# Attention on one NeuronCore: single-bank rings for trial and score products, exponentials 512 wide

## The reference

```
xn = layer_norm(x, norm_w, norm_b)
q = (xn @ q_w + q_b).reshape(Bx, Tx, H, -1)
k = (xn @ k_w + k_b).reshape(Bx, Tx, H, -1)
att = jnp.einsum('bnhl,bmhl->bnmh', q, k)
att = att + (1.0 - mask) * -1000000.0
att = jax.nn.softmax(att, axis=2)
v = ((xn @ v_w + v_b) * src_mask[:, :, None]).reshape(Bx, Tx, H, -1)
y = jnp.einsum('bnmh,bmhl->bnhl', att, v).reshape(Bx, Tx, Dx)
...
h = layer_norm(y, sb_norm_w, sb_norm_b) * (1.0 + scale) + shift
h = jax.nn.silu(h) @ out_w + out_b
return x + h
```

## Time and profile before

| | us |
|---|---|
| median of three runs | 2032.05 |
| the three runs | 2032.08, 2032.05, 2026.07 |
| profiled execution, first to last instruction | 2030.2 |
| lead stretch, 1509.4 to 1572.9 | 63.5 |
| 54 steps with trials, 1572.9 to 1954.2 | 381.3 |
| ten steps without trials, 1954.2 to 2003.8 | 49.6 |
| the end, from 2003.8 | 26.4 |

### The profile page before, as it was taken

How to read it: one execution, slowest core, us unless ns; L and a number is a source line. 1 busy time by engine, 2 the same in 40 slices (tenths; PEclk the granted TensorE clock), 3 DMA queues, 4 the chain that set the end, 5 groups by cost and what they waited for, 6 DMA issues and landing times. The chain is left out here.

```text
span 2030.2 us, 32413 instructions
## 1 busy us (share of the span) xinstructions
PE 1909.2 (94%) x12312; PEld 1341.5 (66%) x12312; DVE 1601.3 (79%) x2109; ACT 1415.3 (70%) x2410; POOL 1047.9 (52%) x603
## 2 busy tenths in 40 slices
PE   6989999999999999989999999899988999999997
PEld 3664999759995799689965998699842222222223
DVE  5565899669995999789976997799969777777642
ACT  3326999379973999699928996998542666665665
POOL 3021799409991599469922997399626000002000
PEclk9989899989999999999999999999988999999998
DMA  5032211102111111011100111111011111111000
GB/s 193 1 102 76 68 58 58 48 27 65 57 52 53 37 58 58 22 44 56 55 11 18 58 58 39 48 58 58 27 24 39 33 31 33 33 33 33 9 22 21
DMA packets 57546, 95.18 MB, mean 47 GB/s; under 512 B 14951, under 2 KB 23559, under 8 KB 55982
## 3 DMA queue, kind: packets, MB, share of 16 engines
q1 hardware_dynamic: 55854, 88.90, 14.3%
q0 software_dynamic: 1536, 4.20, 0.7%
HBM read 73.55 MB, written 6.91 MB: 40 GB/s over the span
## 5 line engine op out<-in xcount | busy, mean ns | idle before, releaser
L973 POOL TENSOR_TENSOR A<-A 128x1024 f32<-128x1024 f32 x384 | 895.7, 2388 | 231.5 <-ACT small L885 161.5
L893 ACT ACTIVATE A<-A,negA 128x512 f32<-128x512 f32 x768 | 549.6, 718 | 30.5 <-DVE A L954 23.6
L954 DVE TENSOR_TENSOR_SCAN A<-A,small,PS 128x512 f32<-128x512 f32 x384 | 453.8, 1258 | 8.2 <-ACT A L893 5.1
L954 DVE TENSOR_TENSOR_SCAN A<-A,PS 128x512 f32<-128x512 f32 x384 | 431.8, 1198 | 21.7 <-PE PS L806 10.9
L831 PE MATMUL PS<-ident,A 128*128 128x128 f32 x3072 | 402.8, 274 | 13.4 <-POOL A L973 10.0
L1499 DVE TENSOR_REDUCE A<-PS 128x1 f32<-128x512 f32 x512 | 324.8, 682 | 101.2 <-PE PS L1486 99.4
L1733 ACT ACTIVATE A<-PS 128x1024 f32<-128x1024 f32 x256 | 260.0, 1023 | 181.7 <-PE PS L1697 179.9
L806 PE MATMUL PS<-A 128*128 128x128 f32 x3072 | 384.8, 277 | 0.2
L806 PEld LDWEIGHTS PS<-A 128*128 128x128 f32 x3072 | 364.0, 193 | 3.6 <-DVE A L954 0.6
L831 PEld LDWEIGHTS PS<-ident,A 128*128 128x128 f32 x3072 | 348.4, 142 | 21.4 <-POOL A L973 13.5
L870 ACT ACTIVATE A<-A,small 128x512 f32<-128x512 f32 x320 | 229.4, 717 | 13.2 <-PE PS L812 13.2
(11 more groups left out here) (194 smaller groups left out, 1841.8 us busy)
## 6 DMA issues: line engine op xcount, KB each, us to landing
A<-scrc SPq DMA_DIRECT2D x192, 256.0 KB, 3.1
A<-A SPq DMA_DIRECT2D x360, 32.0 KB
scr<-A SPq DMA_DIRECT2D x4, 1024.0 KB, 5.0
W<-in_wa SPq DMA_DIRECT2D x2, 1536.0 KB, 9.8
X<-in_x SPq DMA_DIRECT2D x4, 512.0 KB, 5.7
scr<-W SPq DMA_DIRECT2D x128, 1.5 KB
out<-X SPq DMA_DIRECT2D x4, 512.0 KB, 2.9
W<-in_w SPq DMA_DIRECT2D x1, 1984.0 KB, 7.4
```

The source lines that it names most:

```text
L893: e.activation(A_B[i % 4], r.DT[:, dt, ci * 512:(ci + 1) * 512], ACT.Exp, scale=negA[:, r.n, dt * 16 + s:dt * 16 + s + 1]).then_inc(*decay ...
L954: e.tensor_tensor_scan(h, a, u, init, ALU.mult, ALU.add).then_inc(*scanned.up((q, i)))
L973: e.tensor_tensor(h, h, CB[k % 2].unsqueeze(1).broadcast_to([128, 2, 512]), ALU.mult).then_inc(*weighed.up((q, pair)))
```

## The change

The trials get three single banks (0 to 2), the scores three single banks (3 to 5). Every score product of 512 columns now signals for itself, and every Exp is 512 wide: 512 of them in place of 256 of 1024. A weighing block waits for the Exps of its own half c alone, and an Exp waits for the weighing of its own half. In a step the weighing block stands behind the score products of head j = 1 and j = 3, no longer between the first trial and the first score product of that head. The transposed results take two single banks of the trial ring, at the end of the step mt = 1 rather than behind its first head, and VectorE normalises them in two halves, at the end of that step too. VectorE's copy of the upper bank moves from behind head 3 of mt = 0 to behind head 0 of mt = 1. The output projections of the first batch (`tail_due` 2 to 5) take banks of the trial ring, its transposes those of the score ring. In the lead stretch the projections rotate over five banks, not six.

```
-        first, six, doubles = Banks(0, 2), Banks(2, 6), Banks(2, 2, 2)
+        first, five, scores = Banks(0, 3), Banks(3, 5), Banks(3, 3)
...
         def weigh_t(e, w, u, mt, c):
...
                 if mt == 0 and u:
-                    w.wait_ge(*act.at(("lower", u - 1)))
-                    w.wait_ge(*dve.at(("upper", u - 1)))
-                w.wait_ge(*act.at(("weights", u, mt, j)))
+                    w.wait_ge(*(dve.at(("upper", u - 1)) if c else act.at(("lower", u - 1))))
+                w.wait_ge(*act.at(("weights", u, mt, j, c)))
...
         def normalise_t(e, w, u):
-            take(w, ("turned", u), doubles)
...
+            for c in range(2):
+                o = take(w, ("turned", u, c), first)
+                w.wait_ge(*(dve.at(("upper", u)) if c else act.at(("lower", u))))
+                for q in range(4):
+                    t = e.transpose(o[:, q * 128:(q + 1) * 128], PVs[:, c * 512 + q * 128:c * 512 + (q + 1) * 128], ident[:, :])
+                t.then_inc(*pe.up(("turned", u, c)))
...
         def layer3_t(e, w):
...
                     for c in range(2):
                         ahead_t(e, w, LEAD + 32 * u + 4 * mt + j, (c,))
-                        if c == 0:
-                            if last and j % 2:
-                                weigh_t(e, w, *last, j // 2)
-                            take(w, key, doubles)
+                        o = take(w, ("score", u, mt, j, c), scores)
                         w.wait_ge(*transfer(f"max_row{sl}").at(k))
...
-                    t.then_inc(*pe.up(key))
-                    if j == 0 and u and mt == 1:
-                        normalise_t(e, w, u - 1)
+                                 start=True, stop=True).then_inc(*pe.up(("score", u, mt, j, c)))
+                    if last and j % 2:
+                        weigh_t(e, w, *last, j // 2)
+                if u and mt == 1:
+                    normalise_t(e, w, u - 1)
...
         def layer3_s(e, w):
...
-                    e.activation(PX[mt % 2][j], PS[:, i:i + 2, :].rearrange("p a b -> p (a b)"), ACT.Exp).then_inc(*act.up(("weights", u, mt, j)))
-                    banks.give(key, act.now())
+                    for c in range(2):
+                        key = ("score", u, mt, j, c)
+                        w.wait_ge(*pe.at(key))
+                        if step >= 2:
+                            w.wait_ge(*pe.at(("weighed", (step - 2) // 8, (step - 2) % 8, c)))
+                        e.activation(PX[mt % 2][j][:, c * 512:(c + 1) * 512], bank(key), ACT.Exp).then_inc(*act.up(("weights", u, mt, j, c)))
+                        banks.give(key, act.now())
```

More of the change, by code:

```diff
@@ L1347, in program @@
         units = [(b, g) for b in range(NB) for g in range(H // HQ)]
-        first, six, doubles = Banks(0, 2), Banks(2, 6), Banks(2, 2, 2)
-        rings = [banks, first, six, doubles]
+        first, five, scores = Banks(0, 3), Banks(3, 5), Banks(3, 3)
+        rings = [banks, first, five, scores]
         def layer2_done(w):
@@ L1539, in normalise_t @@
         def normalise_t(e, w, u):
-            take(w, ("turned", u), doubles)
[L1541 to L1545, removed]
+            for c in range(2):
[4 more added lines that the diff above has]
+                t.then_inc(*pe.up(("turned", u, c)))
         def normalise_s(e, w, u):
-            w.wait_ge(*pe.at(("weighed", u, TB - 1, 1)))
+            w.wait_ge(*pe.at(("weighed", u, TB - 1, 0)))
             if u:
-                w.wait_ge(*pe.at(("turned", u - 1)))
+                w.wait_ge(*pe.at(("turned", u - 1, 0)))
             e.activation(PVs[:, 0:512], PV[:, 0, :], ACT.Copy).then_inc(*act.up(("lower", u)))
@@ L1560, in normalise_v @@
             b, g = units[u]
[L1561 to L1567, removed]
-            y = Yt[:, b * TB:(b + 1) * TB, HQ * 16 * g:HQ * 16 * (g + 1)].rearrange("p q (j e) -> p q j e", j=HQ)
-            e.tensor_tensor(y, f4[:, :, :, 0:16], RC.unsqueeze(3).broadcast_to([128, TB, HQ, 16]), ALU.mult).then_inc(*dve.up(("y3", u)))
-            banks.give(("turned", u), dve.now())
+            y = Yt[:, b * TB:(b + 1) * TB, HQ * 16 * g:HQ * 16 * (g + 1)].rearrange("p q (j e) -> p q j e", j=HQ)
+            for c in range(2):
+                f4 = bank(("turned", u, c)).rearrange("p (q j e) -> p q j e", j=HQ, e=32)
+                r = RC[:, 4 * c:4 * c + 4, :]
+                w.wait_ge(*pe.at(("turned", u, c)))
+                if u:
+                    w.wait_ge(*dve.at(("y3", u - 1)))
+                e.reciprocal(r, f4[:, :, :, 16]).then_inc(*dve.up())
+                w.wait_ge(*dve.now())
+                e.tensor_tensor(y[:, 4 * c:4 * c + 4], f4[:, :, :, 0:16], r.unsqueeze(3).broadcast_to([128, 4, HQ, 16]), ALU.mult).then_inc(*dve.up(("y3", u)))
+                banks.give(("turned", u, c), dve.now())
         LAST = (range(TB, TB + 4), range(TB + 4, NT))
@@ L1673, in layer3_t @@
             turned_norm_t(e, w, 1)
-            first.follow(banks, [[0], [1]])
-            six.follow(banks, [[i] for i in range(2, 8)])
+            first.follow(banks, [[0], [1], [2]])
+            five.follow(banks, [[i] for i in range(3, 8)])
             todo = front_jobs(1)
@@ L1679, in layer3_t @@
                 if i < len(todo):
-                    front_t(e, w, todo[i], six)
-            doubles.follow(six, [[0, 1], [2, 3]])
-            for key in six.held[4] + six.held[5]:
+                    front_t(e, w, todo[i], five)
+            scores.follow(five, [[0], [1], [2]])
+            for key in five.held[3] + five.held[4]:
                 for mark in banks.given.get(key, []):
```

16 lines of the change are left out of this document (7 added, 9 removed).

## The result

The changed kernel takes 1974.28 us (median of four runs, 1970.25 to 1978.69) against 2030.3 for the kernel before (four runs, 2026.07 to 2032.08): ratio 0.972, 95% interval 0.971 to 0.974. The forecast was 1977.6, in a range of 1967 to 1999. The profiled execution is the one of 1970.25 us, with a span of 1968.5. The stretches of the changed kernel (length, then busy time and count of PE, PEld, DVE, ACT, POOL, granted clock, DMA share and GB/s), which answer to the earlier trace rows: the lead, the 54 steps with trials, the steps without, the end.

What follows compares the result with a forecast made beforehand. TensorE and VectorE were taken to wait for each other through two trial banks. Terms -54.0 + 3.3 + 0.5 - 3.5 - 0.8 = -54.5 us took 2030.2 to 1975.7, plus 1.85 for the median: 1977.6 us, range 1967 to 1999.

Steps and rivals of the forecast that it cites:

- What bounds it: Steps with trials: TensorE and VectorE wait for each other in turn through two trial banks, 0.45 us per half-step.
- The half-step: Two heads in steps with trials: 3.31 to 2.86 us, with margins of 0.16 before T4, 0.25 before S4.
- extra 0.20 in every fourth half-step: Where a head's maxima are closed: the third bank's slack covers it, saving 27 x 0.20 us.
- Exp 512 wide: ScalarE's narrower Exps: 0.50 to 0.60 us from start to start, copy as nearest row, scaled Exp 0.72 as farthest.
- The steps without trials: Ten steps bound by ScalarE: 4.66 to 4.76 us each, +1.0 less some 0.5, net +0.5 us.
- Normalising: Unit ends: TensorE's part stays 0.93 us, trials behind wait 0.55 more; six units +3.3 us, bounds 0 to 8.4.
- The lead: Lead stretch: third bank saves 2.0 us over 22 reduces and some 1.5 of the first; bounds 0 and 5.
- The other 18.4 ... stay as they are: 54 steps' remainder: transposes, first batch's output work, slow start, absent weighing block in step 0; 18.4 us, unchanged.
- SP's queue: Transfers per unit: 43.3 us fit in 47.2, no cost; rival that they set the pace, 1994 us, chance 0.06.
- the clock: Rival, loaded steps: TensorE falls to the lower clock level, half-step some 5.2 us, total 2240 us; chance 0.02.
- a wait that stays: Rival, loaded steps: margins fail and each half-step keeps some 0.14 us, 15 us in all, 1993 us; chance 0.14.
- The end: Last unit's upper half: four transposes, half a reciprocal and half a multiplication in place of whole ones, -0.8 us.

Runs made afterwards that it cites:

- two_trial_banks: The changed kernel with the trial ring cut back to two banks, 512-wide Exps and three score banks kept: 2026.28 us, ratio 0.998 to the kernel before.
- changed_again: The changed kernel itself run once more, on the same chip as later runs: 1974.57 us, ratio 0.973 to the kernel before.
- lead_36: The changed kernel with trials 36 items ahead instead of 40, the lead's operand stacks issued one head later: 1970.41 us, ratio 0.971.
- all_three: The changed kernel with doubled trials in the lead's last 16 items, lead of 36, GpSimd's bias additions moved to steps 3 and 5: 1970.78 us, ratio 0.971.
- free_lead_36: The changed kernel with doubled lead trials, additions in steps 3 and 5, head 6's stack behind head 3's maxima, lead of 36: 1970.36 us, ratio 0.971.
- warm_lead: The changed kernel with each trial product of the lead's last 16 items made twice, into the same bank: 1974.04 us, ratio 0.972.
- free_lead_40: The changed kernel with doubled lead trials, additions in steps 2 and 4, head 6's stack behind head 3's maxima, lead of 40: 1971.05 us, ratio 0.972.

## Why the prediction was right, and where it was off

**What bounds it.** That the two engines waited for each other through two trial banks, 0.45 us a half-step, is shown: with the third bank taken back, the waits return at the same two trials. The forecast's total was right for this reason, and by some luck: terms of 1 to 5 us that it had wrong nearly cancelled.

**The half-step.** Forecast 2.86, measured 2.845; the margins of 0.16 ahead of the fourth trial and 0.25 ahead of the fourth score held. That they were real limits shows in the runs with two score banks and with two activations more. Over 108 half-steps the 0.015 makes 1.6 us more. The extra 0.20 in every fourth half-step went, as forecast, but the third bank, to which the prediction gave it, wasn't needed for it: `two_trial_banks` is without it as well. With three banks and the block in its old place it is gone too, so either of the two seems to be enough (the narrow Exps are in both runs); which of them carried these 5.4 us isn't shown.

**Exp 512 wide.** Taken 0.50 to 0.60 from start to start, measured 0.485, which is the copy's distance to the Exp behind it, 0.48. The row named as the nearest was right to the hundredth; the scaled Exp of the earlier trace rows was a needless upper end. The steps without trials follow from it. ScalarE there:

```profile
1919.47 2.06 ACT L1730 ACTIVATE A<-PS 128x512 f32<-128x512 f32 x4 [0.33 <-PE PS L1693]
1921.87 0.60 ACT L1730 ACTIVATE A<-PS 128x512 f32<-128x512 f32 x1 [0.33 <-PE PS L1693]
```

From 1919.47 to 1921.87 it is 2.40 us a half-step, so 4.8 us a step where 4.76 was forecast.

**Normalising.** The trials behind the transposes wait 0.45 us a unit in place of 0.55. Against the kernel before, where a unit's end took 0.87 (4.18 less 3.31) and not 0.93, it is 0.51 more (1.38, 4.23 less 2.85), so 0.3 us less than forecast in six units.

**The lead.** -5.6 against -3.5: a term that was too small. The last 22 reduces gave the 2.1 expected. VectorE, beside the last projections, which answers to the first line of the earlier trace rows, and later:

```profile
1510.19 9.05 DVE L1499 TENSOR_REDUCE A<-PS 128x1 f32<-128x512 f32 x14 [1.27 <-PE PS L1486]
...
1547.15 8.42 DVE L1499 TENSOR_REDUCE A<-PS 128x1 f32<-128x512 f32 x14
```

Fourteen now follow each other where they came in fours with a gap of 0.27, in the stretches of three heads and not of one: 1.8, 1.1 and 0.6 us, 3.5 in place of 1.5. In `changed_again` the lead is 59.1 long, 4.4 less than before, so about 1 us of the 5.6 is that execution's.

**What was carried over.** "The other 18.4 ... stay as they are" is the step that was off, in parts that nearly cancelled. The first steps grew by 3.4 us (2.4 in `changed_again`), where they ought to have fallen by about 1.1: 4.5 too much. Before, the small operation of VectorE took 0.74 there and the slow products ended at 1576.43, 3.5 us into the steps. A lead that ends earlier moves the steps into GpSimd's additions; where these are moved away, the operation takes 0.17. Why the slow products of the steps are more than before, 21 in one profile and 16 in the other against 8, isn't settled. On the other side, five half-steps in which VectorE also has the first batch's norm got cheaper than forecast. TensorE of the kernel before and of the changed one at the same place:

```profile
1818.03 0.38 PE L1697 MATMUL PS<-A 102*128 102x512 bf16 x1
1819.26 0.39 PE L1486 MATMUL PS<-A 99*128 99x512 bf16 x1 [0.85 <-DVE A L1499]
```

```profile
1779.49 0.38 PE L1693 MATMUL PS<-A 102*128 102x512 bf16 x1
1779.97 0.39 PE L1486 MATMUL PS<-A 99*128 99x512 bf16 x1
```

1.23 from start to start became 0.48. From block to block the five took 20.5 us and take 15.3; 2.9 of that was in the forecast, 2.4 not. The third bank isn't needed for that: with two trial banks the five take 16.6, which is five times 3.31 and nothing extra, and with three banks and the block in its old place 15.5. The half-steps around the Silu gave 1.3 more than forecast, the three with an output projection about as much as forecast (0.1 less, the unit's end that falls among them taken off). Together these come to +0.9, and with the -1.6 and the units' -0.3 to -1.0 against the forecast, where the stretch shows -0.8.

**SP's queue, the clock, a wait that stays.** A unit takes 47 us, 1623.85 to 1670.78 from end to end, as forecast, and no product in the steps of the changed kernel waits for a transfer. The 4 us of slack were enough. Where a shorter lead takes the head start away, TensorE does wait for transfers: 0.69 us in `lead_36`, 1.66 and 1.27 in `all_three`, 0.50 and 1.38 in `free_lead_36`. The clock stayed at the 2.4 GHz level over the loaded steps (0.98 with the slow start). The rule of the Trainium skill that the prediction weighed there ("TensorE: Matmul & The Clock Gate", section "A second HAM failure mode: psum-queue depth-cycling") is not borne out by these rows.

**The end.** The steps without trials and the end gave 2.2 us, where 0.3 was forecast. One part is a wait that the prediction had at 0.5 us at most. In the kernel before, the last weighing blocks wait for the last wide Exps, which end at 2004.97: the block at 2002.31 and the two here end at 2006.93, 4.62 us.

```profile
2003.84 3.09 PE L1534 MATMUL PS<-A,W 128*32 128x512 f32 x16
```

In the changed kernel the last three blocks follow each other without a wait and take 2.78 (the line at 1947.54 above, and 1944.41 in the first profile): 1.8 us less. With the block in its old place they take 3.97, so 1.2 of it is the block's new place and 0.6 the rest of the change. Another part is one execution: the last output projections, the same instructions in both profiles of the changed kernel, first profile and last session:

```profile
1957.27 7.07 PE L265 MATMUL PS<-W,A 128*128 128x256 f32 x32
```

```profile
1960.48 8.15 PE L265 MATMUL PS<-W,A 128*128 128x256 f32 x32
```

The granted clock over them is 1.00 and 0.87: the 1.1 us hang on how soon the clock is back at the higher level. I count this among the scatter.

## What to carry to other kernels

When two engines that are both far from full hand PSUM banks to each other, write the timetable of one period with the starts from the trace and find the first product that needs a bank of its own period: it tells whether one more bank ends the wait, and by what margin. Price a narrower instruction by the nearest operation of the same source, from start to start and not by its length. Parts that are "carried over unchanged" deserve a look of their own where they stand beside a stretch that moves: here they hid errors of 4.5 and 2.4 us with opposite signs.

## What the runs showed of the hardware

A small VectorE operation can wait for GpSimd. The minimum of two 128x8 tiles in SBUF takes 0.17 us, and 2.04 in the changed kernel, where it starts at 1565.46 and ends at 1567.50 while GpSimd's four operations of 2.31 us end at 1567.48. In `warm_lead` it ends at 1570.89 and they at 1570.86. With the additions moved it is at 0.17. The operation is as slow twice more in the lead, where GpSimd works on the operands: 1.62 each in the kernel before, 1.89 and 1.90 at 1519.27 and 1531.12 in the changed one, where a trial behind the first waits 1.32. No run removes these. The reduces from PSUM in between keep their 0.60. The Trainium skill ("SBUF — State Buffer", section "Who interferes with whom") states this: a VectorE instruction with two SBUF inputs and a GpSimd instruction that reads SBUF contend for a shared port pair, which is an exclusive lock. The trace agrees to 0.03 us; I had not looked for it in the lead.

TensorE's products went from the 2.4 to the 1.2 GHz level after a single stop of 2.08 us (`warm_lead`, until 1578) and of 1.66 us (`all_three`, until 1574) just behind the lead. It happens in the loaded steps too: in `free_lead_36` after stops of 0.50 and 1.38 us, within 2.4 us of each other, with a weighing block of 1.94 us behind them:

```profile
1657.74 0.59 PE L1696 MATMUL PS<-A 102*128 102x512 bf16 x1 [1.38 <-DMA A<-scr]
```

Stops of 1.27 us (`all_three`, 1664.59) and 1.30 (the changed kernel, 1837.95) leave the higher level as it is, and so does a small wait in every half-step. Why some stops bring it down and others of nearly the same length don't isn't settled; `free_lead_40`, with no such stop at the start of its steps, shows no slow product in its steps with trials.
